# An eight-head graph attention over sorted edges: the partial sums are kept in PSUM through all chunks, and a node cut by a chunk's border is corrected by one row

## What is computed

```python
def _gat_conv(x, W, att_src, att_dst, bias, src, dst, heads, out_ch, concat):
    h = (x @ W).reshape(n, heads, out_ch)
    a_src = jnp.einsum('nhc,hc->nh', h, att_src)
    a_dst = jnp.einsum('nhc,hc->nh', h, att_dst)
    logits = jax.nn.leaky_relu(a_src[src] + a_dst[dst], NEG_SLOPE)
    m = jax.ops.segment_max(logits, dst, num_segments=n)
    e = jnp.exp(logits - m[dst])
    denom = jax.ops.segment_sum(e, dst, num_segments=n)
    alpha = e / denom[dst]
    msgs = h[src] * alpha[:, :, None]
    out = jax.ops.segment_sum(msgs, dst, num_segments=n)
```

## Time and profile before

| | |
|---|---|
| median of 3 runs | 3260.48 us (3255.64 to 3260.98) |
| the profiled execution | 3254.36 us, of which the span of its instructions is 3252.2 us |
| TensorE, VectorE, ScalarE, GpSimd busy in that span | 86%, 56%, 42%, 28% |
| mean granted TensorE clock | 0.915 of full speed |
| the stage of the change (`edge_chunks`) | 2377.7 to 2944.7 us of the span, some 567 us |

### The profile page before, as it was taken

The page is one execution under the profiler, slowest core; times in us unless marked ns, Lnnn a source line. Parts: engine busy times, 40 slices in busy tenths (PEclk is TensorE's granted clock), DMA queues, the critical chain, the costliest instruction groups (busy, mean ns, idle before and its releaser), DMA issues. The chain is left out here.

```text
span 3252.2 us, 44556 instructions
## 1 busy us (share of the span) xinstructions
PE 2812.0 (86%) x15308; PEld 2176.7 (67%) x15308; DVE 1828.0 (56%) x4352; ACT 1375.2 (42%) x2647; POOL 924.1 (28%) x734
## 2 busy tenths in 40 slices
PE   5777886999996999999999999999866666676997
PEld 3445774677774878778787787887445555564775
DVE  8998657999977541121121113111556666666994
ACT  4574234999996221111111112111353433333896
POOL 6110070000001643223232231331057777740000
PEclk9999997999998999999999999999957777776999
DMA  5333442111002432112122121320243222103200
GB/s 164 137 116 137 192 180 91 42 42 61 27 1 80 187 133 91 66 61 101 61 89 78 61 96 41 117 96 1 68 102 75 63 48 48 39 17 131 82 36 21
DMA packets 90231, 266.52 MB, mean 82 GB/s; under 512 B 22048, under 2 KB 70007, under 8 KB 80311
## 3 DMA queue, kind: packets, MB, share of 16 engines
q1 hardware_dynamic: 74783, 238.32, 19.9%
q0 software_dynamic: 15232, 25.35, 3.7%
HBM read 232.33 MB, written 31.29 MB: 81 GB/s over the span
## 5 line engine op out<-in xcount | busy, mean ns | idle before, releaser
L3109 PE MATMUL psum<-gate_stream,parts 128*128 128x384 f32 (+1 forms) x3600 | 667.7, 344 | 8.6 <-ACT x L3149 4.4
L3109 PEld LDWEIGHTS psum<-gate_stream,parts 128*128 128x128 f32 x3600 | 630.4, 188 | 25.6 <-issue 6.1
L3214 POOL CAST gate_stream<-gate_adj 128x1920 fp32r<-128x1920 f16 (+1 forms) x200 | 371.7, 1866 | 834.9 <-PE psum L3109 824.1
L2467 PE MATMUL psum<-gat_h,gat_pair 128*128 128x129 f32 (+1 forms) x3750 | 542.5, 290 | 17.0 <-DVE gat_pair L2271 15.3
L2467 PEld LDWEIGHTS psum<-gat_h,gat_pair 128*128 128x128 f32 (+1 forms) x3750 | 458.3, 191 | 128.2 <-DVE gat_pair L2271 67.1
L3247 DVE SCALAR_TENSOR_TENSOR gate_work<-psum,bhh,gate_work 128x384 f32<-128x384 f32 (+1 forms) x80 | 50.1, 626 | 779.1 <-PE psum L3056 763.2
L1691 POOL DMA_INDIRECT edge_rows<-edge_table,src_idx x388 | 390.8, 1007 | 166.6 <-issue 121.4
L2271 DVE SCALAR_TENSOR_TENSOR gat_pair<-gat_above,gat_adj 128x512 f32<-128x512 f32 (+3 forms) x525 | 325.2, 619 | 73.7 <-PE psum L2467 35.8
L2371 ACT ACTIVATE psum<-gat_ad_rows,gat_as 128x512 f32<-128x512 f32 (+3 forms) x525 | 334.9, 638 | 16.8
L2380 ACT ACTIVATE gat_above<-psum,gat_as 128x512 f32<-128x512 f32 (+3 forms) x525 | 324.5, 618 | 40.8 <-PE psum L2455 38.4
L2226 DVE SCALAR_TENSOR_TENSOR gat_acc<-gat_adj,gat_q,gat_acc 128x512 f32<-128x512 f16 (+3 forms) x497 | 327.8, 676 | 0.0
(11 more groups left out here) (502 smaller groups left out, 3997.0 us busy)
## 6 DMA issues: line engine op xcount, KB each, us to landing
gate_adj<-adj SPq DMA_DIRECT2D x35, 2400.0 KB, 8.2
gat_adj<-adj SPq DMA_DIRECT2D x8, 3200.0 KB, 10.9
gcn_adj<-adj SPq DMA_DIRECT2D x10, 2400.0 KB, 8.2
adj<-count_stage SPq DMA_DIRECT2D x196, 100.0 KB, 1.7
edge_place_wide<-row_scratch SPq DMA_DIRECT2D x110, 128.0 KB, 3.2
gate_adj<-adj SPq DMA_DIRECT2D x5, 2800.0 KB, 9.1
gcn_adj<-adj SPq DMA_DIRECT2D x2, 3200.0 KB, 10.4
edge_rows<-edge_table,src_idx POOLq DMA_INDIRECT x388
```

What stands on the lines that cost most here:

```text
L2467: mm = e.matmul(ps[0:p, b, a:a + D + 1], pair[:, g % 2, i * P:i * P + p], h1[:, hi, h, :], start=hi == 0 and i % 3 == 0, stop=hi == NT - 1 ...
L3109: mm = e.matmul(ps[:, f, 0:hi - lo], parts[:, t, m, f, :], stream[:, (NGG * i + t // GG) % GR, 0:windows(i), t % GG * W:(t % GG + 1) * W], ...
L3214: e.tensor_copy(stream[:, n % GR, 0:windows(i), :], cols[:, i % 2, 0:windows(i), g * GW:(g + 1) * GW]).then_inc(widened, 1)
```

## The change

The sums of a chunk are no longer taken out, joined and cleared: PSUM is cleared once and the products of all seven chunks add up there. A node whose edges lie wholly in one chunk has one maximum, so nothing has to be joined for it. A node that is cut by a chunk's border (at most one for each border, since edges are sorted) has been summed with the maximum of its first part. Therefore:

- The forward scan of the maxima starts from the last carry of the chunk before (`carry[:, 0:1]`), so that the later part uses a maximum that includes the earlier one.
- The earlier part's row is read out of the copy `part` by a product with one column (`node_of`, `hold`, at the place told by the new register row `part_r`), VectorE computes how far the maximum has risen (`ease_held`, two small instructions between L1859 and L1862), ScalarE takes one more exponential of 8 values, and VectorE makes a row of differences (`fix_held`, three small instructions between the halves of L1862).
- TensorE adds that row to the sums by a product of one partition before the fifth step of the chunk (`HELD_AT`), after a wait for `fixed`. It loads one more register for it in front of the chunk's first product.
- The copy `take` stays in every chunk and waits for `held` instead of `joined`. `join_most` and `join_sums` run once, after the last chunk; `clear` runs once, in chunk 0. In chunks 1 to 5 the order of `find` and `draw` stays, without the joins between them.
- One more tiny copy (`part_r`) is made when the tables are built, and seven semaphores are added.

The diff, cut to its core:

```diff
+                def ease_held(c):
+
+                    e.wait_ge(held, c)
+                    e.wait_ge(falls, 4 * c + 2)
+                    if c > 1:
+                        e.wait_ge(fixed, c - 1)
+                    e.tensor_tensor(ease[:], held_row[:, 72:80], top[0:1, 0, :], ALU.subtract).then_inc(passed, 1)
+                    e.wait_ge(passed, 3 * (c - 1) + 2)
+                    e.tensor_scalar(ease[:], ease[:], 0.0, None, ALU.min).then_inc(passed, 1)
+
+                def fix_held(c):
+
+                    e.wait_ge(eases, c)
+                    if c > 1:
+                        e.wait_ge(fixes, c - 1)
+                    e.scalar_tensor_tensor(fix[:, 0:64].rearrange("p (h c) -> p h c", h=HEADS),
+                                           ease[:].unsqueeze(2).to_broadcast([1, HEADS, 8]), -1.0, held_heads, ALU.add, ALU.mult)
+                    e.scalar_tensor_tensor(fix[:, 64:72], ease[:], -1.0, held_row[:, 64:72], ALU.add, ALU.mult)
+                    e.tensor_scalar(fix[:, 72:SUMS], held_row[:, 72:SUMS], -1.0, None, ALU.mult).then_inc(fixed, 1)
...
+                    if c:
+                        e.wait_ge(carries_up, c)
+                        e.tensor_copy(carry[:, 0:1], carry[:, KP:KP + 1]).then_inc(passed, 1)
+                        e.wait_ge(passed, 3 * (c - 1) + 1)
...
-                    e.tensor_tensor_scan(carry[:, 1:n + 1], self.rows_start[:, steps(c)], ends[0:HEADS, 0, 0:n], -BIG,
+                    e.tensor_tensor_scan(carry[:, 1:n + 1], self.rows_start[:, steps(c)], ends[0:HEADS, 0, 0:n], carry[:, 0:1],
...
+                    if c:
+                        ease_held(c)
                     e.wait_ge(weights, c + 1)
                     for at in (slice(0, half), slice(half, n)):
                         e.tensor_tensor(by_head(row(c)[:, at, 0:64]), by_head(row(c)[:, at, 0:64]), channels(weight[:, at]),
                                         ALU.mult).then_inc(marks, 1)
+                        if c and at.start == 0:
+                            fix_held(c)
                     ahead = of_chunk[c + 1]
                     if ahead:
-                        find([(ahead[0], 0, HEAD)])
-                    if c:
-                        join_most(c - 1)
-                    if ahead:
-                        find([(ahead[0], HEAD, NT)])
-                    if c:
-                        join_sums(c - 1)
+                        find([(ahead[0], 0, NT)])
                     for m, then in zip(ahead, ahead[1:]):
-                        find([(then, 0, HEAD)])
+                        find([(then, 0, RING)])
                         draw(m)
-                        find([(then, HEAD, NT)])
+                        find([(then, RING, NT)])
                     if ahead:
                         draw(ahead[-1])
-                join_most(end)
-                join_sums(end)
+                join_most()
+                join_sums()
...
-                        e.wait_ge(joined, 2 * c)
+                        e.wait_ge(held, c)
...
+                    if c:
+                        e.wait_ge(node_up, c)
+                        e.copy(node_col[:], node_up_to).then_inc(node_in, 1)
...
                     if c:
-                        ease_off(c - 1)
+                        e.wait_ge(passed, 3 * c)
+                        e.activation(ease[:], ease[:], ACT.Exp).then_inc(eases, 1)
                 take(end)
-                ease_off(end)
+                ease_off()
...
-                def clear(c):
-
-                    if c == 0:
-                        e.wait_ge(packed, len(pieces))
-                    e.wait_ge(carried_in, 2 * c + 1)
+                def node_of(c):
+
+                    e.wait_ge(hots, 2 * share * c + 2)
+                    if c > 1:
+                        e.wait_ge(node_in, c - 1)
+                    e.transpose(node_up_to, hot[0:1, 0, :], self.ident[0:1, 0:1]).then_inc(node_up, 1)
+
+                def hold(c):
+
+                    e.load(part_regs, self.part_r[0:1, c:c + 1])
+                    at = e.snap(part_regs[0], min_val=0, max_val=SUMS * (NT - 1))
+                    e.wait_ge(node_in, c)
+                    e.wait_ge(taken, c)
+                    if c > 1:
+                        e.wait_ge(fixed, c - 1)
+                    e.matmul(held_row, node_col[:], flat_part[:, bass.ds(at, SUMS)], start=True, stop=True).then_inc(held, 1)
+
+                def clear():
+
+                    e.wait_ge(packed, len(pieces))
+                    e.wait_ge(carried_in, 1)
...
+                    if c:
+                        e.load(first_regs, out_r[0:1, first_step[c]:first_step[c] + 1])
+                        to_first = e.snap(first_regs[0], min_val=0, max_val=4 * 512)
...
+                        if c and s == HELD_AT:
+                            e.wait_ge(fixed, c)
+                            e.matmul(flat[:, bass.ds(to_first, SUMS)], hot[0:1, 0, :], fix[:], start=False, stop=False,
+                                     skip_group_check=True).then_inc(fixes, 1)
...
                     line_up(c)
+                    if c:
+                        node_of(c)
                     ends_of(c)
                     carries_of(c)
+                    if c:
+                        hold(c)
                     peaks_of(c)
-                    clear(c)
+                    if c == 0:
+                        clear()
                     sums(c)
```

More of the change, by code:

```diff
@@ L1615, in edge_chunks @@
         gone = self.sb("edge_gone", [P, NT], F32, st)
+        node_col = self.sb("edge_node_col", [P, 1], F32, st)
+        fix = self.sb("edge_fix", [1, SUMS], F32, st)
+        ease = self.sb("edge_ease", [1, HEADS], F32, st)
         fall = self.sb("edge_fall", [P, 2, NT, HEADS], F32, st)
@@ L1619, in edge_chunks @@
                  "second", "peaks_up", "falls", "weights", "filled", "marks", "hots", "summed", "taken", "present", "eased", "joined",
-                 "copied", "spread", "packed", "ones", "pulled", "drawn", "split")
+                 "copied", "spread", "packed", "ones", "pulled", "drawn", "split", "passed", "node_up", "node_in", "held", "eases", "fixed", "fixes")
         (hots_t, products, added, logits, lines, first, ends_up, carries, carries_up, carried_in,
          second, peaks_up, falls, weights, filled, marks, hots, summed, taken, present, eased, joined,
-         copied, spread, packed, ones, pulled, drawn, split) = (
+         copied, spread, packed, ones, pulled, drawn, split, passed, node_up, node_in, held, eases, fixed, fixes) = (
             nc.alloc_semaphore("edge_" + n) for n in names)
@@ L1636, in edge_chunks @@
         size, first_step = CHUNKS, CHUNK_AT
+        assert all(at == KP * c for c, at in enumerate(first_step))
         by_pool = [size[c] - DRAWN[c] for c in range(end + 1)]
@@ L1732, in draw, with join_most, join_sums @@
                     inst.then_inc(drawn, 1)
-                def join_most(c):
-                    e.wait_ge(taken, c + 1)
+                def join_most():
+                    e.wait_ge(taken, end + 1)
                     e.tensor_scalar(gone[:], part[:, :, SUMS - 1], -1.0, BIG, ALU.add, ALU.mult).then_inc(present, 1)
-                    e.wait_ge(present, 4 * c + 1)
-                    if c:
-                        e.wait_ge(joined, 2 * c)
+                    e.wait_ge(present, 1)
                     e.tensor_tensor(fall[:, 1], part[:, :, 72:80], per_node(gone[:]), ALU.add).then_inc(present, 1)
[L1742 to L1750, removed]
-                    if c:
-                        e.wait_ge(joined, 2 * c)
+                    e.wait_ge(present, 2)
+                    e.tensor_tensor(high[:, 1], high[:, 0], fall[:, 1], ALU.max).then_inc(present, 1)
+                    e.wait_ge(present, 3)
+                    e.tensor_tensor(fall[:, 0], high[:, 0], high[:, 1], ALU.subtract)
+                    e.tensor_tensor(fall[:, 1], fall[:, 1], high[:, 1], ALU.subtract).then_inc(present, 1)
+                def join_sums():
+                    e.wait_ge(eased, 1)
                     e.tensor_tensor(by_head(acc[:, :, 0:64]), by_head(acc[:, :, 0:64]), channels(fall[:, 0]), ALU.mult)
@@ L2077, in _ @@
                         e.wait_ge(drawn, of_chunk[c + 1][-1] + 1)
-                for r in out_regs + tab_regs:
+                for r in out_regs + tab_regs + part_regs + first_regs:
                     e.free_register(r)
@@ L2082, in edge_chunks @@
             second, peaks_up, falls, weights, filled, marks, hots, summed, taken, present, eased, joined,
-            copied, spread, packed, ones, pulled, drawn, split, begun] + fetched + place_in + src_in)
+            copied, spread, packed, ones, pulled, drawn, split, passed, node_up, node_in, held, eases, fixed, fixes, begun] + fetched + place_in + src_in)
         st.close()
```

23 lines of the change are left out of this document (14 added, 9 removed).

## The result

| | before | after |
|---|---|---|
| median, first measurement | 3255.77 us (5 runs) | 3242.41 us (5 runs, 3230.83 to 3244.77) |
| ratio after to before | | 0.9949, 95% interval 0.9938 to 0.9959 |
| second measurement | 3255.99 us (9 runs) | 3243.01 us (6 runs), ratio 0.9965 (0.9952 to 0.9977) |
| profiled execution, its span | 3254.36, 3252.2 us | 3243.15, 3241.4 us |

The forecast was 3246 us, 14.8 us under the 3260.48 of the three early runs of the kernel before. The measured 3242.41 is 3.6 us under the forecast, since the kernel before itself takes 4.7 us less in its five runs than in those three. By the medians the change takes off 13.4 and 13.0 us; by the ratios 16.6 and 11.4.

The account below looks back on a forecast made before the run. GpSimd's gathers were taken to bound the kernel. From the early median of 3260.5 us, 15.9 us less for gathers no longer stretched and 1.1 more for added last-chunk instructions gave 3246 us, range 3240 to 3252.

Parts of the forecast that it names:

- The bound: Eight-head attention stage: GpSimd's gathers pace the chunks, some 70 us each; TensorE and VectorE are ready 2 to 5 us earlier.
- The relief: Chunks 1 to 5: removing five joins ends their sets of three long gathers, saving 15.9 us, bounds 0 and 17.5.
- rival 1: No relief: joins do not hold the gathers, or other two-SBUF-operand VectorE instructions meet them instead; 3262 us, chance 0.09.
- The leg: TensorE and VectorE's own work per chunk, L1798 until ready for the next: some 67 us, against 70 of gathers.
- The additions: New instructions: 0 in chunks 1 to 5, 1.1 us in the last chunk, bounds 0.5 and 2.5.
- the register: One more register load before TensorE's first product of the sums: 0.3 us in the last chunk, bounds 0 and 0.7.
- The correcting product: TensorE's extra product in the sums, after the wait for `fixed`: no stall, costs one step, 0.44 us in last chunk.
- the clock: TensorE's clock in the last chunk's sums: taken as 0; +4.5 us if it never rises, -2 if 4 us earlier.
- The sum: Whole kernel: profiled 3254.36 - 15.9 + 1.1 = 3239.6 us; from the median 3260.5 - 14.8 = 3245.7, predicted as 3246.
- Rival 2: TensorE and VectorE's work, not gathers, comes last, through handshakes of 1 us or more; 3253 or 3260 us, chance 0.07.

## Why the prediction was right, and where it was off

- **The bound.** Right on the chips where it was made: the gathers set the pace before and after.
- **The relief.** Forecast 15.9 us of gathers' time. The five sets are gone, and the busy time fell by 14.5: other gathers met other VectorE instructions, five of them for 1.29 to 1.54 us, and gave 1.3 us back. That is what rival 1 had in its second half, in small. From the first gather to the last it was 511.3 us (2378.30 to 2889.55) and is 496.8 (2379.94 to 2876.76). So 14.4 us was the true size of this term.
- **The leg.** Forecast some 67 us, measured 66.98 in chunk 1, with chunk 0 as the model. That it comes so close is partly luck: chunks 2 to 4 have 67.4 to 67.9 us, and the second measurement 68.1 to 68.5. Its spare time went into the wait, 22.2 us in sum after 22.8.
- **The additions.** Forecast 1.1 us in the last chunk. `ease_held` delayed the weights' product by 0.36 us (0.4 forecast): 16.25 us from L1823 to L1893, 15.89 before. From there to the first sum it is 3.36 us, 2.92 before: 0.44, which I put down to the register (0.3). The five profiles of changed kernels have 3.36 to 3.38 there, and the kernel before without joins 2.93. The correcting product is in the 23.2 us of sums, and the clock that rose 1.1 us sooner paid for it. In all L1823 to the first copy took 42.9 us instead of 42.2: 0.7. Off by 0.4, through the clock, of which I had taken 0.
- **The sum.** Forecast -14.8 us for the profiled execution, measured -11.2 (by the span -10.9). The stage gave 14.4 less 0.7, some 13.8. The missing 2.9 of the span are outside it: the first gather begins 1.6 us later, and what follows the last join takes 1.3 us longer. The seven profiles with the quicker times put the first gather anywhere from 2378.3 to 2386.1, so such a shift belongs to a single execution, not to the change. The medians, 13.4 and 13.0 us, agree with the stage. That the absolute time came within 3.6 us of the forecast owes something to two misses of opposite sign: the kernel before was 4.7 us quicker than the three runs had it, and the gain 1.4 us smaller.
- **The Trainium skill.** Its inference that a tensor_tensor with two SBUF inputs does not stall the making of descriptors (SBUF — State Buffer, section "Who interferes with whom") is against the runs: 376.0 us of gathers with reductions in that place, 386.2 with tensor_tensor. The same section's rule that tensor_reduce never contends agrees with them.
- **Rival 2** named the leg as what might come last. Here it did not, with 3 us to spare as forecast; on the slower chips it does, and there the gain is zero, the size that this rival had. Its mechanism, handshakes of 1 us or more, is not what makes the leg long there: those are TensorE's pauses. I had taken the bound as one of the kernel. It is one of the kernel on a chip.

## What to carry to other kernels

When gathers are issued by GpSimd one after the other, look for VectorE's long instructions with two SBUF operands beside them: a gather that begins well inside one lasts until 0.8 us after its end, here 3.3 us lost for three. Move such work off, or let one operand come from PSUM or be a reduction, before shortening VectorE's own leg. The second and fourth gather of every version still lose 3.1 us together under two such instructions of 128x1800 elements (L1762 and L1768); moving those was not tried. And before a long stretch of thin products (here 81 columns each), see which clock it runs at: filling the gaps of the last chunk gave some 5 us in the sums, beside the change's 13.

## What the runs showed of the hardware that I had not expected

- Two chips ran the same program 417 us slower (3672 against 3255 us), with most of the extra time in TensorE's idle time of "issue" while gathers run (442 us against 50), and changed which engine comes last, so that one edit was worth 13 us on one chip and 0 on the other.
- A 16-bit comparison of VectorE with one tensor operand, 0.34 us long, holds a gather as the long two-operand instructions do: the gather ends 0.82 us after it, or after the last of three in a row (1.54 us instead of 0.94).
- GpSimd has two pauses of 2.0 to 2.1 us, after the gathers number 173 and 285, in the changed kernel as in the one before. They are 3.2 and 2.5 us with the two-operand instructions, 3.4 and 3.1 with the reductions, and 2.1 and 3.0 with the added products of TensorE. They came with no other engine's release; their cause is open.
